# Attention and a top-2 expert layer on one core: expert results stored by token and by lower or higher expert, x kept in SBUF, q and k parts in three transfers

## The reference

```python
x = x + xattn(layernorm(x), ctx, ctx, ...)     # 16 heads of 8, rope, each query sees 65 keys
x = x + ffn(layernorm(x), router_w, w1, w2)    # and ffn(u) adds its own input u once more
# ffn(u): probs = softmax(u @ router_w.T); the best 2 of 8 experts of each token, weights renormalised
#   an expert takes its first 1281 (token, choice) pairs in token order; later ones are dropped
#   expert: silu(u @ w1[e]) @ w2[e]; a token's result is the weighted sum of its two experts'
```

## Time and profile before

| | us |
|---|---|
| median of 3 runs | 521.02 (520.77 to 524.34) |
| profiled execution, its own time | 516.97 |
| span of that execution, first to last instruction | 515.0 |
| busy in the span: PE / DVE / ACT / POOL | 409.9 / 361.2 / 261.9 / 322.9 |

### The profile page before, as it was taken

One profiled execution on the slowest core, in us unless ns is written; L12 is line 12 of the kernel. 1 busy time (PEld: TensorE's weight loads), 2 busy tenths in 40 slices (PEclk: granted clock), 3 DMA queues, 4 the chain that ended last, 5 costly groups with the idle time before them and its releaser, 6 DMA issues.

```text
span 515.0 us, 16333 instructions
## 1 busy us (share of the span) xinstructions
PE 409.9 (80%) x5659; PEld 322.7 (63%) x5659; DVE 361.2 (70%) x1138; ACT 261.9 (51%) x587; POOL 322.9 (63%) x250
## 2 busy tenths in 40 slices
PE   3553598989999999999999953889989999989500
PEld 2342466767777777777777742478877877877400
DVE  4786367787988989888888763077778678777300
ACT  1111254555555665555665632198868768768000
POOL 7442023175777767777665587207688888888882
PEclk9997789998999999999999995999999999999855
DMA  8986876777788887888988445535565565543331
GB/s 190 235 206 172 219 196 154 200 181 162 180 183 180 196 195 170 184 184 184 208 184 167 67 44 83 114 98 111 84 123 76 85 130 74 86 38 36 36 35 12
DMA packets 89046, 70.32 MB, mean 137 GB/s; under 512 B 8992, under 2 KB 75808, under 8 KB 88480
## 3 DMA queue, kind: packets, MB, share of 16 engines
q1 hardware_dynamic: 68208, 60.09, 45.8%
q0 software_dynamic: 20784, 9.53, 19.9%
HBM read 38.85 MB, written 30.74 MB: 135 GB/s over the span
## 4 chain that ended last, share of the span: by engine, by line
SPq 25%; PE 24%; DMA 15%; issue 14%; POOL 10%; ACT 7%; DVE 4%; DVEq 0%; POOLq 0%; ACTq 0%
PE bank L479 20%; DMA k_scratch<-parts 6%; SPq L378 5%; DMA k_pack<-k_scratch 5%; SPq L376 5%; SPq L358 4%; POOL queues L1406 4%; POOL out L1486 4%; SPq L363 4%; ACT hidp L918 3%; ACT hid L914 3%; DMA q_pack<-maxT 2%; PE bank L703 2%; SPq L388 2%; DMA queues<-rows,index 1%
## 5 line engine op out<-in xcount | busy, mean ns | idle before, releaser
L1486 POOL DMA_INDIRECT out<-ys,row_token x80 | 129.0, 1613 | 50.0 <-issue 47.0
L943 DVE TENSOR_REDUCE maxima<-bank 128x4 f32<-128x512 f32 x128 | 87.7, 687 | 35.5 <-PE bank L479 31.6
L1406 POOL DMA_INDIRECT queues<-rows,index x64 | 100.8, 1576 | 18.0 <-issue 17.7
L806 ACT ACTIVATE probs<-bank 128x512 f32<-128x512 f32 x128 | 76.4, 597 | 54.6 <-PE bank L479 54.1
L1354 DVE TENSOR_TENSOR hidp<-hid,hidp 128x512 fp32r<-128x512 f32 (+1 forms) x96 | 57.2, 604 | 25.7 <-ACT hidp L918 24.5
L479 PE MATMUL bank<-k_pack,q_pack 128*64 128x128 bf16 x1024 | 55.1, 233 | 15.7 <-DMA k_pack<-k_scratch 15.1
L479 PE MATMUL bank<-q_pack,k_pack 128*128 128x64 bf16 x1024 | 53.1, 196 | 14.8 <-DMA q_pack<-maxT 14.3
L479 PE MATMUL bank<-xTp,w1p 128*128 128x512 f32 (+1 forms) x288 | 61.1, 361 | 2.8 <-DVE xTp L1216 2.8
L479 PE MATMUL bank<-hidp,w2p 128*128 128x512 f32 (+1 forms) x288 | 62.2, 365 | 0.0
L479 PE MATMUL bank<-probs,v_sb 128*32 128x64 f32 x2048 | 56.0, 226 | 5.7 <-ACT csb L813 3.0
L914 ACT ACTIVATE hid<-bank 128x512 f32<-128x512 f32 (+1 forms) x96 | 54.2, 564 | 10.1 <-PE bank L479 9.9
(11 more groups left out here) (148 smaller groups left out, 691.1 us busy)
## 6 DMA issues: line engine op xcount, KB each, us to landing
k_pack<-k_scratch SPq DMA_DIRECT2D x64, 192.0 KB, 3.8
q_pack<-q_scratch SPq DMA_DIRECT2D x64, 128.0 KB, 3.1
queues<-empty SPq DMA_DIRECT2D x8, 682.5 KB, 7.6
xs<-queues SPq DMA_DIRECT2D x7, 650.0 KB
q_scratch<-parts SPq DMA_DIRECT2D x16, 192.0 KB
k_scratch<-parts SPq DMA_DIRECT2D x16, 192.0 KB
xin<-in_x SPq DMA_DIRECT2D x16, 128.0 KB, 3.1
cin<-in_ctx SPq DMA_DIRECT2D x16, 128.0 KB
```

The lines of the kernel that those rows point to most:

```text
L806: nc.scalar.activation(probs[u % 2][:], bb[u % 2][:], ACT.Exp).then_inc(S["prob_s"], 1)
L943: v.reduce_max(maxima[par][:, 4 * hg:4 * hg + 4, i2], ab[u % 2][:].rearrange("p (h c) -> p h c", c=P), AX).then_inc(S["max_s"], 1)
L1406: g.indirect_dma_start(queues, bass.IndirectOffsetOnAxis(ap=index[par][:, n:n + 1], axis=0), rows[par][:, n // TILES, n % TILES, :], None, ...
L1486: g.indirect_dma_start(out, bass.IndirectOffsetOnAxis(ap=row_token[par][0:n, t:t + 1], axis=0), ys[c][0:n, col // P, :], None, compute_op= ...
```

## The change

Five things are done.

1. **Results by token and lower or higher expert.** A new HBM tensor `results` has 4096 rows for the result of a token's lower-numbered expert and 4096 for that of the higher one. Every place is written once, so the scatter is a plain indirect write, not an addition; all waits on the expert before, `find_meetings`, `meeting_rows`, `add_meetings` and all `left_*` work go. An expert now has 11 scatters, the last of 4 rows. The scatter of token rows into the queues becomes a plain write too. `results` is cleared by eight writes of 512 KB that SP issues in steps 14 to 17.
2. **The sum at the end.** After all scatters of experts 0 to 6 have landed SP loads the 4096 lower results (four transfers of 512 KB) and DVE adds them to the base. After the last scatter SP loads the higher ones in eight transfers of 256 KB, DVE adds each piece, SP writes each to `out`.
3. **x stays in SBUF** in `xkept`: loaded once, two batches per transfer, it takes on the attention result and then the base in place. The residual load (L415) and the write of the base (L408) go, and the clearing of the spare rows of `out`.
4. **Parts in three transfers.** The parts lie as k3, k2, k1, q1, q2, q3 in one tile and the two scratch tensors are one, so that two transfers carry the products of parts 1 and 2 after part 2 and one carries the other half after part 3.
5. **All steps are written out**; there is no hardware loop. DVE gets two small instructions in routing (`later`, and the tag made from it).

```diff
-        FIRST, LOOP, END, LAST = -4, 2, 10, 18
+        FIRST, LAST = -4, 18
         def steps(eng, body):
-            for k in range(FIRST, LOOP):
-                body(k, k % 2, k // 2)
-            with eng.Fori(0, (END - LOOP) // 2) as n:
...
+            for k in range(FIRST, LAST):
                 body(k, k % 2, k // 2)
...
-                    after(sp, "part3", 1, j)
-                    for part, at, times in ((0, 0, 3), (1, 3, 2), (2, 5, 1)):
-                        sp.dma_start(to[:, at:at + times, :],
-                                     parts[:, part, 0, :].unsqueeze(1).to_broadcast([P, times, TOKENS])
...
+                    after(sp, "part2", 1, j)
+                    apart(sp, "past_sp")
+                    sp.dma_start(to[:, 1:12:4, :], parts[:, 1:4, :]).then_inc(S["scr_w"], 16)
+                    sp.dma_start(to[:, 3:12:4, :], parts[:, 2:5, :]).then_inc(S["scr_w"], 16)
                 else:
                     after(sp, "part3", 1, j)
+                    sp.dma_start(to[:, 0:12:2, :], parts[:, 0:6, :]).then_inc(S["scr_w"], 16)
...
-                if on(k - 2):
-                    after(sp, "base_s", 1, k - 2)
-                    sp.dma_start(out[bass.ds((k - 2) * TOKENS, TOKENS), :]...
-                    sp.dma_start(xres[par][:], x[k, :, :].rearrange("(t p) c -> p t c", p=P)).then_inc(S["xr_in"], 16)
...
+                if isinstance(k, int) and k >= BATCHES - 2:
+                    for n in range(2 * (k - BATCHES + 2), 2 * (k - BATCHES + 3)):
+                        sp.dma_start(results[n * CLEAR:(n + 1) * CLEAR, :]...
...
+            added_all(sp, EXPERTS - 1)
+            for n in range(BATCHES // QUARTER):
+                sp.dma_start(early[:, n * QUARTER:(n + 1) * QUARTER, :, :]..., results[at:at + QUARTER * TOKENS, :]...
             added_all(sp, EXPERTS)
+            for n in range(pieces):
+                sp.dma_start(late[n][:], results[at:at + PIECE * TOKENS, :]...
+            for n in range(pieces):
+                sp.wait_ge(S["summed"], n + 1)
+                sp.dma_start(out[at:at + PIECE * TOKENS, :]..., late[n][:]
...
-                    if c == 0 and meets(e):
-                        pool.wait_ge(S["added0"], e * (16 * len(full_tiles(0))))
-                        pool.wait_ge(S["paired"], 3 * (e - 1))
-                    elif c == 0 and e > 0:
-                        added_all(pool, e)
...
-                    for t, col, n in full_tiles(c):
+                    for t, col, n in tiles_of(c):
-                        g.indirect_dma_start(out, bass.IndirectOffsetOnAxis(
+                        g.indirect_dma_start(results, bass.IndirectOffsetOnAxis(
                             ap=row_token[par][0:n, t:t + 1], axis=0),
-                            ys[c][0:n, col // P, :], None, compute_op=ALU.add).then_inc(S[f"added{c}"], 16)
+                            ys[c][0:n, col // P, :], None).then_inc(S[f"added{c}"], 16)
```

More of the change, by code:

```diff
@@ L68 @@
 TAIL = USED - CAPACITY + 1
-LEFT = EXPERTS * TAIL
+PLACES = 2 * ALL
+PIECE = 2
+QUARTER = 4
+CLEAR = 1024
 CHUNKS = [512, 512, USED - 1024]
@@ L127, in build @@
         tag_step = sb("tag_step", [P, 2, TILES])
+        tok = two("tok", [P, 2, TILES])
+        later = sb("later", [P, TILES])
         half_neg = sb("half_neg", [P, TILES])
@@ L161, in build @@
         rows = two("rows", [P, 2, TILES, ROW])
-        base = two("base", [P, TILES, DIM])
         xn2T = sb("xn2T", [P, TOKENS])
@@ L174, in build @@
         mask_rows = sb("mask_rows", [P, 3, TOKENS], BF16)
-        empty = sb("empty", [INIT_P, INIT_R, ROW])
+        with ExitStack() as clearing:
+            empty = clearing.enter_context(nc.sbuf_tensor("empty", [INIT_P, INIT_R, ROW], F32))
+        early = sb("early", [P, BATCHES, TILES, DIM])
         xs = two("xs", [P, 11, ROW])
@@ L459, in _ @@
             load_expert(0, 0)
-            for e in range(EXPERTS):
-                sp.dma_start(left[TAIL * e:TAIL * (e + 1), :], queues[e * QUEUE + 10 * P:e * QUEUE + USED, DIM:DIM + 2]
-                             ).then_inc(S["left_in"], 16)
             def body2(e, par):
@@ L589, in inputs_across @@
                     after(pe, "xn1_s", 2, j)
-                    after(pe, "c_in", 16, j)
+                    if j == 1:
+                        pe.wait_ge(S["c_second"], 16)
+                    else:
+                        pe.wait_ge(S["c_in"], 16 * max(j, 1))
                     for t in range(TILES):
@@ L1091, in route @@
                     after(dve, "indexed", 2, j)
+                    after(dve, "tok_s", 1, j - 1)
+                    apart(dve, "past_dve")
+                    v.tensor_tensor(later[:], top_index[:, :, 0], top_index[:, :, 1], ALU.is_gt).then_inc(S["later_s"], 1)
                     done(v.tensor_tensor(chosen[:],
@@ L1099, in route @@
                     v.tensor_tensor(both16[:], chosen[:, 0, :, :], chosen[:, 1, :, :], ALU.add).then_inc(S["both_s"], 1)
+                    after(dve, "later_s", 1, j)
+                    apart(dve, "past_dve")
+                    after(dve, "tok_step", 1, j)
+                    v.scalar_tensor_tensor(rows[par][:, :, :, DIM + 1], later[:].unsqueeze(1).to_broadcast([P, 2, TILES]),
+                                           float(ALL), tok[par][:], ALU.mult, ALU.add).then_inc(S["tok_s"], 1)
                 elif n == 4:
```

334 lines of the change are left out of this document (120 added, 214 removed).

## The result

The new kernel takes 491.78 us (median of four runs, 487.03 to 495.62) where the kernel before took 521.90 beside it: a ratio of 0.939, with a 95% interval of 0.934 to 0.944, so it is faster. On another chip, six runs gave 489.55 and 0.945 (0.941 to 0.948). The profiled execution took 489.78 with a span of 488.0, 27 us less than the 515.0 of before. I had forecast 513 with a range from 493 to 530: the direction was right, the gain was more than three times what I had summed, and the time lies just under the range.

The account below looks back on a forecast made before the run. SP's issuing was taken to bound attention, POOL beside PE the experts. Early steps -9.0, later -5.6, hand-over -0.8, scatters -6.0 and end +13.6 sum to -7.8 us; put on the median 521.02 that gave 513, range 493 to 530.

Parts of the forecast that it names:

- What bounds the kernel: Whole kernel: SP's issuing sets attention's steps, PE and DVE 1 us behind; in the experts POOL and PE bound side by side.
- I take 1.72, just below the middle: Experts: plain scatters follow each other after 1.72 us instead of 1.92, saving 6.0 us over the chain.
- My lower bound of 1.60: Experts: the shortest scatter spacing allowed for, if all work by the row vanished, saving 15.6 us.
- POOL stays the bound: Experts: PE's period falls to 16.4 us, under POOL's 18.7, so PE and DVE savings count nothing.
- Scatter far cheaper: Rival, experts: spacing under 1.48, PE's 16.4 bounds an expert, 28.4 us saved in all, 493; chance 0.17.
- Attention: Attention steps: SP relieved of 3.1 us a step, saving 9.0 us in the early steps and 5.6 in the later.
- The six early steps: Start of attention: 9.0 us saved, bounds 4 and 15, with only SP's 3.1 us a step certain.
- the entry of the loop: Attention, step at 109.1, 17.7 us long, where the loop is entered: 2.7 us saved.
- the nine later ones: Later attention steps: PE next in line, 14.9 us a step, 5.6 us saved, bounds 1.5 and 8.
- Hand-over: Between attention and experts: cheaper scatters save 1.6 us, clearing results costs 0.8, net 0.8 saved.
- The end: After the last scatter: 1.8 landing, 17.6 late half, 4.6 after final landing, 24.0 against 10.4; cost 13.6 us.
- The additions beside the last scatters: Last scatters: four large DVE additions beside them cost up to 2.0 us by the shared-port rule.

Follow-up runs that it names:

- e1: The new kernel with its 88 scatters into results accumulating again: 529.16 us, 1.017 of the kernel before.
- e4: The kernel before with its loop over the steps written out, all else as before: 1.004 of the kernel before.
- e14: The new kernel loading only one of two copies of k from the third batch on, 384 KB less a step: 485.38 us, 0.935 of the kernel before.
- e6: The new kernel with SP's second x load and 128 KB write put back in each step: 500.56 us, 0.963 of the kernel before.
- e8: The new kernel with the eight clears of results issued one a step in steps 4 to 11 of attention: 495.36 us, 0.950 of the kernel before.
- e2: The new kernel with its 64 scatters into the queues accumulating again, those into results plain: 496.80 us.
- e12: The new kernel with the eight clears of results issued behind the first rows and weights of the experts: 486.11 us, 0.936 of the kernel before.
- e16: The new kernel without reading or adding the higher experts' results, scatters into results accumulating: 7.0 us from last scatter to end of span.
- e13: The new kernel without reading or adding the higher experts' results, scatters plain: 10.4 us from last scatter to end of span.

## Why the prediction was off

- *What bounds the kernel* was read rightly: SP in the steps, POOL and PE side by side in the experts, "so work taken from PE alone gives nothing". `e1` shows just that: with the removed work and the old price nothing is gained.
- *The step that failed* is "I take 1.72, just below the middle". One plain scatter follows another after 1.26 by the median and 1.37 on the mean. My lower bound of 1.60 came from the price by the row of an accumulating scatter and kept its fixed 1.22 whole; I had written that the fixed part may fall as well, and left it out because no row showed it. It did fall: a scatter of four rows takes 0.89, where `e1`, accumulating, has 1.34. That 1.34 also shows the 1.22 as misread: the 1.59 and 1.35 of the earlier trace rows, from which I took the price by the row, are scatters of different rows, of 130 and of 128 numbers.
- With it fell *POOL stays the bound* and the choice to count PE's and DVE's savings at nothing. My own figure for PE's period, 16.4, was right (16.56), and the spacing fell under 1.48, where I had the bound change hands; no run tries a price near that point. The rival *Scatter far cheaper* forecast a chain of 131 and 28.4 us in all; measured were 131.7 and 27.0. For the chain that is the mechanism; that the total agrees to 1.4 is luck, since against that rival's sum attention gained 3.1 less, the hand-over 4.8 less, and the end cost 6.6 less. I gave it 0.17 and set the range's lower end on its time, 493, without leaving room below.
- *Attention.* The six early steps came out at 9.4 for 9.0, which is partly luck: on the mean of the eleven executions it is 7.5, the first two steps gained 0.4 where I had 1.8, and the 2.7 that I put down to the entry of the loop is not the loop's (`e4`). For the nine later ones I took 14.9 a step and got 15.3 (137.6 / 9), because the transfers stand beside PE (`e14`, `e6`, `e8`), a bound that I had not put into the sum. Over all executions the gain in attention is 9 to 15 us (244.3 to 250.1 against 235.1 on the mean), for which the sum had 14.6.
- *Hand-over.* The cheaper scatters gave about 5 us and not 1.6 (`e2`). The clears took back more than the 0.8 I had charged: between 274.1 and 291.1 SP spent 14.3 us on issuing them, and DVE waited 3.6 us for scatters of rows to land beside them, a wait that `e8` and `e12` do not have. The ten matmuls, which had been hidden behind the load of the rows, ended 2 us after it; no run shows these 2 us as gained.
- *The end.* Three terms of 24.0 were too long. A scatter lands 1.2 after its end, not 1.8. The late half takes from 471.7 to about 487.5, 15.8 and not 17.6; the estimate that I had worked out from the Trainium skill, "DMA: Bandwidth & Descriptors", section "Anatomy of one DMA", was 13.6, so the measured time lies between the two. (That section has its two figures from transfers issued by GpSimd; those of the late half are issued by SP.) And the 4.6 that I let follow the final landing is POOL's DRAIN of 4.65, which follows the last scatter and not the last transfer: in the new kernel it lies beside the late half.
- *The additions beside the last scatters.* Four scatters there took 1.40, 1.28, 1.87 and 1.49 where others take 0.96: 2.2 us more, near the 2.0 that I had put to the rule in the Trainium skill, "SBUF — State Buffer", section "SBUF: two separate sides", with a size from my own rows. Each of the four overlaps one of DVE's additions. The early loads alone do not do it: the scatter at 458.62 took 0.96 while they moved 342 GB/s and DVE was idle.

```profile
458.60:459.60 1.00, 0.00 (x0) 0.00 (x0) 0.00 (x0) 0.00 (x0) 0.96 (x1) 1.00 1.14 342
```

But in `e16` the accumulating scatters beside the same additions took 1.56 each, as the others there do, so not every scatter beside an addition grows longer, and the trace does not show why.

## What to carry to other kernels

When a change replaces an operation by one of another kind, the rows of the old kind give no lower bound: work out at which price the bound changes hands, and let the range reach beyond the case on its far side. Where two engines stand side by side, price the two edits together and each alone, since neither need show a gain without the other. What a program still does after its last scatter can hide a good part of what is added there, so an end is measured with the added work left out.

## What the hardware showed that was not expected

- An indirect write of 128 rows costs POOL 0.968 us plain and 1.543 accumulating, and most of the difference is fixed: four rows cost 0.89 and 1.34. On the DMA engines 152 plain scatters are 4864 packets, 32 each, and 6.0% of the 16 engines' time; 145 accumulating ones were 20784, 143 each, and 19.9%, for the same bytes.
- After the last scatter of a program 7.0 us pass when those of the experts accumulate and 10.4 when they are plain, most of it with nothing moving (`e16`, `e13`). It is a DRAIN of POOL, of 5.01 and 7.59 us, and work on other engines and queues can lie beside it. Why it is longer after plain ones is not settled.
- Traffic alone moves a step that PE fills to 98%: 384 KB less in a step gives 0.3 us in the later steps (`e14`). 512 KB more, with one issue of SP more, costs 0.8 (`e8`).
